# Every gather of a recommendation kernel waits until GpSimd is through with the gather before it

## What is computed

```python
field_idx = jnp.arange(N_FIELDS)
sparse_embed = emb_tables[field_idx[None, :], x_sparse]      # B x 26 x 64
z = sparse_embed.reshape(B, N_FIELDS * K)
gram = jnp.einsum('bik,bjk->bij', sparse_embed, sparse_embed)
iu, ju = jnp.triu_indices(N_FIELDS, k=1)
inner = gram[:, iu, ju]                                      # 325 products
dnn_in = jnp.concatenate([x_dense, z, inner], axis=-1)       # B x 2002
h = jax.nn.relu(dnn_in @ w1 + b1)
out = jax.nn.sigmoid(h @ w2 + b2)
```

## Time and profile before

| | |
|---|---|
| time, median of 3 runs | 448.31 us (448.2 to 449.79) |
| span of the profiled execution | 584.9 us |
| TensorE busy in it | 436.1 us, 75% of the span |
| GpSimd busy in it | 215.9 us, of which 214.9 are the 208 gathers |
| VectorE, ScalarE busy | 316.2 us, 274.3 us |

### The profile page before, as it was taken

One profiled execution on the slowest core, in us unless ns is written; L12 is line 12 of the kernel. 1 busy time (PEld: TensorE's weight loads), 2 busy tenths in 40 slices (PEclk: granted clock), 3 DMA queues, 4 the chain that ended last, 5 costly groups with the idle time before them and its releaser, 6 DMA issues.

```text
span 584.9 us, 6070 instructions
## 1 busy us (share of the span) xinstructions
PE 436.1 (75%) x2011; PEld 355.6 (61%) x2011; DVE 316.2 (54%) x670; ACT 274.3 (47%) x443; POOL 215.9 (37%) x215
## 2 busy tenths in 40 slices
PE   7814040999787899445999932059989999999997
PEld 7613030777675777334887721047867888887885
DVE  4510010565638698302679830049886478989542
ACT  2400020383689867315986630029543368864330
POOL 6777772477723437770005777700000000000000
PEclk9967575899999999755999975568989999999999
DMA  7643351569634857441356863312666373465730
GB/s 232 154 71 62 26 98 12 155 160 277 189 78 117 201 156 226 85 61 34 113 156 206 214 153 26 62 36 62 152 206 219 102 244 106 141 193 196 258 90 0
DMA packets 29455, 77.96 MB, mean 133 GB/s; under 512 B 8480, under 2 KB 8488, under 8 KB 29424
## 3 DMA queue, kind: packets, MB, share of 16 engines
q1 hardware_dynamic: 22768, 70.75, 38.8%
q0 software_dynamic: 6656, 6.83, 11.4%
HBM read 77.55 MB, written 0.00 MB: 133 GB/s over the span
## 4 chain that ended last, share of the span: by engine, by line
PE 42%; another core or an unknown queue 18%; ACT 15%; issue 12%; DVE 9%; DMA 2%; SPq 1%; POOL 1%; DVEq 0%; ACTq 0%
PE ps L562 13%; PE ps L574 12%; PE ps L564 12%; ACT w_hi L627 4%; DVE w_lo L733 3%; ACT gram L662 3%; DVE weighed L837 2%; PE ps L522 2%; ACT pair_u L648 2%; ACT pair_v L651 2%; PE ps L508 2%; DMA w_raw<-in_L_rec_w_dram 1%; ACT pair_v L650 1%; SPq L392 1%
## 5 line engine op out<-in xcount | busy, mean ns | idle before, releaser
L451 POOL DMA_INDIRECT z<-in_L_rec_emb_tables_dram,idx x208 | 214.9, 1033 | 162.6 <-PE ps L508 99.4
L562 PE MATMUL ps<-w_hi,x_hi 128*128 128x502 f32 (+1 forms) x512 | 212.5, 415 | 73.2 <-issue 46.5
L564 PE MATMUL ps<-w_lo,x_hi 128*128 128x502 f32 (+1 forms) x480 | 194.0, 404 | 4.6 <-issue 4.6
L733 DVE TENSOR_TENSOR w_lo<-w_raw,w_hi 128x1002 fp32r<-128x1002 f32 x120 | 141.2, 1200 | 100.8 <-ACT w_hi L627 51.6
L627 ACT CAST w_hi<-w_raw 128x1002 fp32r<-128x1002 f32 x128 | 128.7, 1033 | 83.6 <-remote 27.7
L562 PEld LDWEIGHTS ps<-w_hi,x_hi 128*128 128x128 f32 x512 | 101.1, 197 | 102.9 <-issue 55.6
L574 PE MATMUL ps<-w_hi,x_lo 128*128 128x502 f32 (+1 forms) x480 | 142.8, 403 | 4.0 <-issue 3.1
L564 PEld LDWEIGHTS ps<-w_lo,x_hi 128*128 128x128 f32 x480 | 95.1, 198 | 21.4 <-issue 4.2
L574 PEld LDWEIGHTS ps<-w_hi,x_lo 128*128 128x128 f32 x480 | 92.8, 196 | 23.9 <-issue 4.3
L635 ACT CAST x_hi<-ps 128x256 fp32r<-128x256 f32 (+2 forms) x36 | 16.2, 472 | 121.6 <-PE ps L508 62.2
L662 ACT COPY gram<-ps 32x104 f32<-32x104 f32 x160 | 39.7, 248 | 54.3 <-remote 32.7
(11 more groups left out here) (46 smaller groups left out, 184.4 us busy)
## 6 DMA issues: line engine op xcount, KB each, us to landing
w_raw<-in_L_rec_w_dram SPq DMA_DIRECT2D x112, 501.0 KB
w_raw<-in_L_rec_w_dram SPq DMA_DIRECT2D x24, 250.5 KB
w_raw<-in_L_rec_w_dram SPq DMA_DIRECT2D x8, 438.4 KB
z<-in_L_rec_emb_tables_dram,idx POOLq DMA_INDIRECT x208
w_raw<-in_L_rec_w_dram SPq DMA_DIRECT2D x24, 62.6 KB
w2b<-in_L_rec_w_dram SPq DMA_DIRECT2D x1, 501.0 KB
w2b<-in_L_rec_w_dram SPq DMA_DIRECT2D x1, 500.0 KB
w_raw<-in_L_rec_w_dram SPq DMA_DIRECT2D x8, 50.9 KB
```

The source lines that it names most:

```text
L451: pool.indirect_dma_start(out=z[:, t % 2, K * f:K * (f + 1)], out_offset=None, in_=emb_rows, in_offset=bass.IndirectOffsetOnAxis(ap=idx[:, ...
L562: nc.tensor.matmul(into(c, t), hi, of_w(w_hi, c, k), start=first, stop=False)
L564: nc.tensor.matmul(into(c, t), hi, of_w(w_lo, c, k), start=False, stop=False)
L733: nc.vector.tensor_tensor(low, raw(n)[at, :], high, ALU.subtract).then_inc(w_lo_done, 1)
```

## The change

A new semaphore, `described`, is raised by one through `engine_sem` when GpSimd itself is through with a gather: its descriptors are written and its transfer is set off. The data need not have landed. Before each gather but the first, GpSimd waits until `described` has reached the number of gathers issued so far. So 207 of the 208 gathers get a wait on the gather directly ahead of them. The order of the instructions on every engine stays as it was, and no other engine waits on the new semaphore.

```diff
@@ -313,6 +313,7 @@
         idx_step = sem("idx_step")
         idx_done = sem("idx_done")
         w2_zero = sem("w2_zero")
+        described = sem("described")
@@ -448,11 +449,16 @@
             def gather(t, k, done):
                 for f in (2 * k, 2 * k + 1):
+                    if gathers:
+                        pool.wait_ge(described, len(gathers))
+                    gathers.append((t, f))
                     pool.indirect_dma_start(
                         out=z[:, t % 2, K * f:K * (f + 1)], out_offset=None, in_=emb_rows,
                         in_offset=bass.IndirectOffsetOnAxis(ap=idx[:, t, f:f + 1], axis=0),
+                        engine_sem=described,
                     ).then_inc(done, 16)
 
+            gathers = []
             pool.wait_ge(idx_done, 1)
```

## The result

The changed kernel takes 457.43 us (455.74 to 463.05), the kernel before 449.05 us in the same series; the ratio is 1.0151, 95% interval 1.0086 to 1.0217. The run of 463.05 us fell in the chip's slow state and is not in the ratio. A second series of the same kernel gave 1.0161 (1.0118 to 1.0203). The prediction was 461.0 us and slower. So the sign and somewhat over half of the size came true (1.5 to 1.6% for a forecast of 2.8%), but, as the experiments show, by another mechanism than the one that was summed.

The account below looks back on a forecast made before the run. TensorE was taken to bound the kernel, with the gathers right behind it. At J(1, 4), 92 x 0.16 us of waits less 2.0 us of slack gave 12.7 us; 448.3 + 12.7 = 461.0 us, range 447.0 to 493 us.

Parts of the forecast that it names:

- Taking the standstills out: Removing profile stretches where TensorE, VectorE and ScalarE stand still while GpSimd gathers, 51.4 us before 102 us.
- the slope: Extra cost per gather adds up along GpSimd's stream and delays TensorE: at J(1, 4), 92 x 0.16 less 2.0 us.
- The pace of the gathers: On GpSimd with all engines working, one gather every 1.42 us: 1.12 us of record and 0.30 us between two.
- The slack at J(1, 4): TensorE wants J(1, 4) at 138.6 us and gather 92 is there at 136.6: 2.0 us to spare.
- rival C: Gathers already hold TensorE up and their gap falls from 0.30 to 0.27 us: 2.8 us faster, 445.5 us; chance 0.05.
- The price of a wait, x: Time from a gather's record end until GpSimd is through with it: taken as 0.19 us, bounds 0 and 0.9.
- e: Extra cost of each waiting gather on GpSimd, x + 0.27 - 0.30 us: taken as 0.16 us.
- rival A: GpSimd raises the semaphore at the record's end or within hundredths, so the gap doesn't grow: 448 us; chance 0.25.
- the queued gap: On GpSimd, 0.30 us between gathers already queued; about 0.11 taken as the next one's start, at most 0.19 as tail.
- theory R: From the experiments: a separate wait on the gather just before stops GpSimd's sequencer, exposing 0.53 us of preparation; gap 0.77 us.
- The later gathers: After J(1, 5), 38 gathers for tiles 4 and 5 take 62 us and are wanted 78 us later, hiding the cost.
- The margin over tiles 6 and 7: The 52 gathers for tiles 6 and 7 take 85 us and are wanted 111 us later, hiding the cost.

Follow-up runs that it names:

- own_each: The changed kernel with a needless second wait at each of 207 gathers, putting the wait on `described` in an instruction of its own; 528.37 us, ratio 1.1737.
- base: The kernel before, unchanged, run again for a profile without standstills; span 448.5 us at a device time of 450.28 us.
- inner_only: The changed kernel without the new wait at the first gather of each batch, keeping the 184 inside the batches; ratio 0.9962 to the kernel before.
- two_waits_each: The kernel before with two needless waits, on semaphores raised early, at every one of the 208 gathers; ratio 1.0035.
- foreign_wait: The kernel before with a needless second wait, on a semaphore raised early, at the first gather of each batch; ratio 0.9982.
- foreign_pair1: The kernel before with a needless second wait, on a semaphore raised early, at the 7 batch starts of pair 1 alone; ratio 1.0027.
- swapped: The changed kernel with all 207 waits, the two at each batch start in the other order so the gather carries `described`; ratio 0.9974 to the kernel before.
- one_back: The changed kernel with the new wait at batch starts alone, on the gather before the last, in its own instruction; ratio 1.0015 to the kernel before.
- starts_only: The changed kernel with the new wait only at the 23 batch starts, none inside the batches; ratio 1.0165 to the kernel before.

## Why the prediction was right, and where it was wrong

**Taking the standstills out: right.** The span without them is 448.5 us. The reading that gathers stand right behind TensorE, against the 37% of the earlier trace rows, gave the sign, and own_each confirms the slope.

**The pace of the gathers: right within a few per cent.** 1.42 us was used; in base gather 92 is recorded by 130.5 us, where the working gave 3.9 + 92 x 1.42 - 0.3 = 134.2.

**The slack at J(1, 4): wrong, by two errors.** TensorE wanted J(1, 4) earlier than worked out: 138.6 us was the sum, and base has it at 135.2 us after a wait of 3.4, so it was wanted at 131.8. And the 2.4 us from the end of a record to its use, read at gather 8, did not hold there. In base gather 92 is the first of these rows and J(1, 4) the second, 4.7 us from record to use:

```profile
129.56 0.94 POOL L451 DMA_INDIRECT z<-in_L_rec_emb_tables_dram,idx  x1 [0.30 <-issue]
...
135.20 1.11 PE L508 MATMUL ps<-ident,z 128*128 128x128 f32 x4 [3.40 <-DMA z<-in_L_rec_emb_tables_dram,idx]
```

The longer way to the use ate 2.3 of the 3.7 us that the faster pace had gained. In place of a slack of 2.0 us TensorE waited there 3.4 us in base, 2.6 in inner_only and 2.2 in two_waits_each, and 0.3 us or less in foreign_wait, foreign_pair1, swapped and one_back. So rival C's condition, that gathers hold TensorE up already, was met in some executions; its gap of 0.27 us was not.

**The price of a wait, x: wrong.** This is the term that the forecast rested on. The semaphore rises 0.01 us after the record, so the lower bound, x = 0, is the true value, and e is 0.00 and not 0.16 us inside a batch. By the prediction's own sum that gives rival A, no change. What the prediction took from the queued gap (at most 0.19 us of tail) rested on the thought that a gather released by a semaphore must start later than one that stands in the queue. A wait that the gather carries itself left the gap at 0.30 us, as without a wait; by theory R the gather stands in the queue prepared. The argument held against A, that a queue would then save nothing, fell with it: by theory R the queue saves the 0.53 us of preparation, which such a wait does not touch. The Trainium skill's page Perfetto Trace Analysis, section DMA Instruction — SWDGE (GPSIMD), was right here where the sum was not: it puts the recorded end at the last descriptor, and the 0.01 us to the semaphore agree. The estimate by its page DMA: Bandwidth & Descriptors, 0.4 us for x, is not borne out.

**A term that was missing: the batch starts.** The prediction spoke of 207 equal waits and did not ask where a second wait on the same instruction goes.
**The later gathers: wrong.** For tiles 4 and 5 the prediction let 38 gathers start at J(1, 5), with 16 us to spare. But GpSimd was still behind there: in base the record of gather 104 ends at 147.0 us and J(1, 5) comes at 150.7, so some 50 gathers were left and not 38. The record of gather 156 ends at 219.7, its data can be used 2.4 us later, and the last transposes start at 228.9: 6.9 us of room for the last two, and more for those before. The 7.0 us of 15 batch starts are as much as this room, and the 12.4 us by which gather 156 was late in the changed kernel's profile are more; the largest waits of that profile are there. The margin over tiles 6 and 7 held.

**The size.** 12.7 us were forecast and about 7 us measured, by the ratios. Two errors had opposite signs: 92 x 0.16 = 14.7 us that do not exist, and 7.0 us of batch starts that were not in the sum. That the number came close was luck. Had the 23 starts been written as in swapped, the same reasoning would have forecast the same 461 us, and the measured ratio of swapped is 0.9974.

## What to carry to other kernels

A wait is not priced by what it waits for alone, but by where it stands: carried by the gather itself and fulfilled when its predecessor ends it cost nothing, as an instruction of its own on the instruction just issued it took away the sequencer's run-ahead, 0.47 us each time. Where an instruction needs two waits, write the one that is fulfilled last so that the instruction itself carries it, or leave one instruction of distance; and look into the built program for wait instructions that were not there before. Both are shown here for gathers on GpSimd alone. And a profile with standstills must be cleared of them before an engine that ran on through them is called idle.

## What the runs showed that I had not expected

The sequencer of GpSimd ran 12 gathers ahead (foreign_wait) and prepared one in about 0.53 us (two_waits_each), less than half of what a gather then takes (1.25 us and more).

In the kernels where nearly every gather waits on `described` (the changed kernel, inner_only, swapped), eleven single gathers from number 146 on start after 0.55 to 0.60 us and number 114 after 0.88 us, though they are no batch starts; in starts_only, one_back and two_waits_each they are not there. What they are is open. They add 3.6 us to the stream, of which 1.4 us (gathers 114, 146, 150 and 154) lie ahead of gather 156. inner_only and swapped have them and are not slower than the kernel before, so no run shows a cost of them. In own_each the same gathers stand out too, with 0.97 to 1.63 us where the others have 0.77.
